# A graph network's first layer: the edge-score products with 128 moving columns instead of 64 and 1

## The reference

```
h = x @ W_w + W_b
row, col = (edge_index[0], edge_index[1])
e = h[row] @ a_src + h[col] @ a_dst + a_b
e = jax.nn.leaky_relu(e, negative_slope=0.01)
attention = jax.nn.softmax(e, axis=0)
msg = attention * h[col]
out = jax.ops.segment_sum(msg, row, num_segments=N_NODES)
```

## Time and profile before

| | |
|---|---|
| time before, median of 3 runs | 11837.31 us (11834.0 to 11841.89) |
| the profiled execution | 11841.19 us, span 11839.4 us |
| first weight load of line 556 to the last sum of this stage | 217.8 to 929.8 us |
| mean granted clock over the span | 0.742 |

### The profile page before, as it was taken

One profiled execution on the slowest core, in us unless ns is written; L12 is line 12 of the kernel. 1 busy time (PEld: TensorE's weight loads), 2 busy tenths in 40 slices (PEclk: granted clock), 3 DMA queues, 4 the chain that ended last, 5 costly groups with the idle time before them and its releaser, 6 DMA issues. The chain is left out here.

```text
span 11839.4 us, 182004 instructions
## 1 busy us (share of the span) xinstructions
PE 7849.9 (66%) x39163; PEld 6599.3 (56%) x39164; DVE 7062.0 (60%) x13587; ACT 2661.2 (22%) x8800; POOL 6678.2 (56%) x6703
## 2 busy tenths in 40 slices
PE   4995444437886377764654777563788778877886
PEld 3995444426775355542433666462566556655665
DVE  4445454444444289995675666566566656665666
ACT  1331000001111200004651000131333333333333
POOL 0006888846775077762322777330677667766776
PEclk6555666655555799997986666675899889988998
DMA  3114555543221167764532444330444344434444
GB/s 108 38 39 85 95 96 97 95 91 84 81 81 55 24 224 244 245 217 102 157 115 61 153 152 153 105 111 27 138 154 154 124 138 154 150 128 138 154 150 137
DMA packets 828292, 1435.96 MB, mean 121 GB/s; under 512 B 182864, under 2 KB 494268, under 8 KB 787760
## 3 DMA queue, kind: packets, MB, share of 16 engines
q1 hardware_dynamic: 531136, 981.94, 25.7%
q0 software_dynamic: 297072, 453.23, 17.0%
HBM read 1115.44 MB, written 320.07 MB: 121 GB/s over the span
## 5 line engine op out<-in xcount | busy, mean ns | idle before, releaser
L1614 POOL DMA_INDIRECT T<-gather_d,srci x2508 | 2459.3, 981 | 1263.4 <-issue 755.6
L827 POOL DMA_INDIRECT added_d<-T,slots x832 | 1296.3, 1558 | 281.5 <-issue 219.7
L1198 PE MATMUL PS<-T,ident 128*128 128x256 f32 (+1 forms) x3328 | 1069.2, 411 | 453.8 <-DMA T<-wide_d,srci 244.7
L1147 POOL DMA_INDIRECT T<-wide_d,srci x832 | 860.4, 1034 | 673.5 <-PEq L71 420.1
L1147 POOL DMA_INDIRECT T<-gather_d,srci x832 | 820.1, 986 | 531.7 <-PEq L71 278.3
L1196 PE MATMUL PS<-T 128*128 x3328 | 1004.3, 392 | 139.9 <-issue 98.5
L1418 PE MATMUL PS<-T 128*128 128x260 f32 (+1 forms) x3328 | 806.7, 403 | 424.0 <-DVEq L1471 349.6
L1198 PEld LDWEIGHTS PS<-T,ident 128*128 128x128 f32 x3328 | 672.4, 236 | 705.7 <-DMA T<-wide_d,srci 347.6
L940 POOL DMA_INDIRECT T<-gather_d,srci x832 | 792.8, 953 | 439.1 <-issue 253.7
L1397 POOL TENSOR_TENSOR T<-T,LG 128x256 f32<-128x256 f32 (+1 forms) x840 | 429.6, 532 | 998.6 <-PE PS L1418 753.7
L1418 PEld LDWEIGHTS PS<-T 128*128 128x128 f32 x3328 | 634.5, 240 | 596.2 <-DVEq L1471 329.8
(11 more groups left out here) (252 smaller groups left out, 16011.4 us busy)
## 6 DMA issues: line engine op xcount, KB each, us to landing
T<-quads_d SPq DMA_DIRECT2D x315, 1024.0 KB
T<-edge_rows_d SPq DMA_DIRECT2D x210, 512.0 KB
edge_rows_d<-T SPq DMA_DIRECT2D x209, 512.0 KB, 2.8
T<-onehot_t_d SPq DMA_DIRECT2D x416, 256.0 KB
T<-gather_d,srci POOLq DMA_INDIRECT x4172, 2.6
T<-edge_rows_d SPq DMA_DIRECT2D x210, 256.0 KB
onehot_t_d<-T SPq DMA_DIRECT2D x208, 256.0 KB, 3.4
edge_rows_d<-T SPq DMA_DIRECT2D x208, 256.0 KB, 2.1
```

The source lines that it names most:

```text
L827: gp.indirect_dma_start(added_d[u][:, :], bass.IndirectOffsetOnAxis(ap=slots[:, k:k + 1], axis=0), part(OUT[r], u), None, compute_op=ALU.a ...
L1147: gp.indirect_dma_start(part(R[n % RING], u, width), None, table[:, :], bass.IndirectOffsetOnAxis(ap=srci[:, k:k + 1], axis=0)).then_inc(r ...
L1198: last = T_.matmul(spot(i, u), ident[:, :], part(R[r], u, width), start=False, stop=True)
L1614: gp.indirect_dma_start(part(R[n % RING], u), None, gather_d[:, :], bass.IndirectOffsetOnAxis(ap=srci[:, k:k + 1], axis=0)).then_inc(rows_ ...
```

## The change

Both products of a step get 128 moving columns. The first takes all 128 columns of `S2` (the upper ones are zero in columns 49 to 127). The second takes 128 columns of `LG` from the step's block on. It is written from column 64 of the place in PSUM on, over the upper half of what the first wrote; its first column is the one that is used. A place in PSUM grows from 65 to 256 columns for a step, so four groups now take all eight banks. The mask reads 4 x 65 numbers with a stride of 256 in place of 260 in a row. Weights, loads, one-hot matrices, `pick`, sums and the number of instructions stay.

```
-        S2 = W[:, 5 * DIM:5 * DIM + LOW]
+        S2 = W[:, 5 * DIM:6 * DIM]
...
-            tcols = LG[:, 2 * ALL:2 * ALL + BLOCKS]
+            tcols = LG[:, 2 * ALL:2 * ALL + 2 * P]
...
-            spot = lambda r, u: bank(r)[:, u * both:(u + 1) * both]
+            room = 2 * P
+            spot = lambda r, u: PS[:, (r * GROUP + u) * room:(r * GROUP + u + 1) * room]
...
-                                T_.matmul(spot(r, u)[:, 0:LOW], part(LH[r], u), S2[:, 0:LOW], start=True, stop=True)
-                                last = T_.matmul(spot(r, u)[:, LOW:both], part(OT[r], u), tcols[:, bass.ds(bs[e % 2 * GROUP + u], 1)], start=True, stop=True)
+                                T_.matmul(spot(r, u)[:, 0:P], part(LH[r], u), S2, start=True, stop=True)
+                                last = T_.matmul(spot(r, u)[:, LOW:LOW + P], part(OT[r], u), tcols[:, bass.ds(bs[e % 2 * GROUP + u], P)], start=True, stop=True)
...
-                        V.tensor_tensor(PR[r % 2], bank(r)[:, 0:GROUP * both], EQ[r % 2], ALU.mult).then_inc(masked.h, 1)
+                        V.tensor_tensor(split(PR[r % 2], both), split(PS[:, r * GROUP * room:(r + 1) * GROUP * room], room)[:, :, 0:both], split(EQ[r % 2], both), ALU.mult).then_inc(masked.h, 1)
```

## The result

The changed kernel takes 11500.2 us (median of 4 runs, 11483.2 to 11508.1) against 11835.7 for the kernel before (4 runs, 11830.4 to 11841.9): a ratio of 0.9714 by the means of the runs, interval 0.9698 to 0.9731, and 335 us less by the medians. The direction and the main mechanism (the clock rises) are as forecast. The size is not quite: 317 us were predicted, and 11520 lies above what the interval allows (0.9731 x 11837 = 11519). The result sits on the lower edge of the range. The profiled execution took 11504.85 us, span 11503.1.

A forecast was written before the change was run, and what follows sets the result against it. TensorE's weight-load pitch at granted clock 0.50 was taken to bound the edge-score stage; 319.4 us gained at the high clock less 2.4 for its rise left -317, from 11837.3 to 11520 us, range 11498 to 11590.

The forecast's parts named there:

- What bounds the stage, and what 128 columns cost: Edge scores: TensorE alone sets the time, 0.213 us a record by its weight load; columns up to 128 are free.
- The clock rises: Edge scores: dense 128-column products with 128 rows lift TensorE's granted clock from 0.50 to 1.00.
- The group at the high clock: Edge scores: TensorE takes 1.784 us per group of 16 records, saving 1.628; VectorE, ScalarE and loads fit beneath.
- the upper bound of 2.26 us a group: Edge scores: pace if TensorE's instruction queue, at 56 ns an instruction, set it; 91 us more.
- The start of the stage: Until 266 us writes of zeros crowd DMA: 2.67 us a group, 16 groups done; stage's last product 319.4 us earlier.
- the prediction's own sign: Edge scores: the prediction counts as wrong if the stretch before 266 us holds many more than 16 groups.
- The rise of the clock: Edge scores: some 5 us at the low clock after TensorE's waits, half of them lost, taking 2.4 us off the gain.
- The rest does not move: Everything after the edge scores keeps its time, as nothing later shares the stage's data or its clock.
- another engine takes over: Rival: TensorE's queue or VectorE's waits set 1.9 to 2.26 us a group, 22 to 91 us more; chance 0.14.
- the clock stays: Rival: granted clock remains 0.50 in the edge scores and nothing changes, 11837 us; chance 0.05.
- the slower case: Rival: clock remains low and 128-column products take 0.251 us a record, 126 us more, 11963; chance 0.02.
- The variant without any hold-up by the zeros: Rival: all 208 groups run at 1.784 us, -335 us, 11502; counted as lower edge of the main case, 0.78.

The follow-up runs named there:

- e1: Changed kernel's PSUM places and strided mask, but products of 64 and 1 columns as before; 11851.7 us against 11855.3 for the kernel before.
- e2: Changed kernel with 128 columns in the source product only, the target product having 1; 11838.9 us against 11855.3 for the kernel before.
- e4: Changed kernel with 128 columns in both products but only 64 of the 128 rows; 11864.7 us against 11855.3 for the kernel before.
- e6: Changed kernel with the 64-row product of layer 1's edge stage given 128 rows, added ones zero; 12874.9 us against 12863.9 for the changed kernel.
- e0: The changed kernel run again, nothing altered; 12863.9 us against 13186.0 for the kernel before.
- e7: Changed kernel with the zeros cleared and written while layer 0's node product runs; 12832.6 us against 12831.2 for the changed kernel.
- e11: Changed kernel with two writes of zeros started with layer 0's node product, two with VectorE's sums behind it; 11510.7 us against 11518.1 for the changed kernel.
- e9: Changed kernel without TensorE's loads of block numbers, always taking block 0's columns; 12824.5 us against 12831.2 for the changed kernel.
- e3: Changed kernel with 128 columns in the target product only, the source product having 64; 11520.7 us against 11855.3 for the kernel before.

## Why the prediction was right or wrong

**What bounds the stage, and what 128 columns cost**: right. At 0.50 the pitch of a record is 0.213 us for 1, 64 and 128 columns (e1, e2, e4), at the high level 0.112 for 64 and 128 (predicted 0.1115). That it is the weight load's pitch fits, but no run changes the 128 columns of the load itself.

**The clock rises**: right, and the reason given (what moves, and not the busy share) is borne out by e1 to e4. That layer 1's stage spoke against it only through its 64 rows was a guess in the prediction; e4 shows that half the rows hold the clock at 0.50, and e6 that with full rows it leaves 0.50 in spite of the gaps. The gap as a sole cause falls; that it costs part of the way (0.69 and not 1.00) is not excluded.

**The group at the high clock**: right. 1.79 us against 1.784; no other engine took over. VectorE keeps 0.23 us. TensorE's queue is no bound where a register load takes 0.59 us, and the upper bound of 2.26 us a group did not come up.

**The start of the stage**: this step failed. "49 GB/s, so a pair of 0.262 MB takes 5.35 us, 2.67 us a group. That replaces 1.784 as the pace" made the stage 608.5 - 217.8 = 390.7 us, and 393.1 with the 2.4 us for the clock, from the first load to the end of the last product. It took 605.3 - 226.3 = 379.0. In e0, whose stage began at 218.9 us, 22 groups had been masked by 266 us, and not 16; from the first of these masks to the last are (265.86 - 222.78) / 21 = 2.05 us a group. By the prediction's own sign (many more than 16 groups before 266 us) this step was wrong.

It went wrong in two ways. First, the sum of 16 groups counts only the tables that arrive once the stage runs. The ring's four pairs, eight groups, had landed before it. DMA of the kernel before, 205 to 215 us, with eight loads of 128 KB:

```profile
q1 hardware_dynamic: 1152, 1.05, 36.0%
T<-step_at_d SPq DMA_DIRECT2D x4, 128.0 KB, 3.8
T<-step_lo_d SPq DMA_DIRECT2D x4, 128.0 KB, 4.1
```

With them, and with the prediction's own rate, (1.05 + 2.1) / 0.262 = 12 pairs or 24 groups are there by 266 us. The other 184 take 328.3 us, and the stage comes to 594.3 - 217.8 + 2.4 = 378.9 us. That this meets the 379.0 measured so closely is in part luck, since the rate was off too.

Second, the rate of 49 GB/s came from the earlier trace rows, 0.49 MB in ten us, and the queue could carry more. The changed kernel drew 0.60 from as crowded engines, between 235 and 245 us:

```profile
q0 software_dynamic: 667, 2.67, 82.2%
q1 hardware_dynamic: 655, 0.60, 20.0%
```

The kernel before needs a pair every 6.8 us, 0.38 MB in ten us. From 225 to 275 us it drew 0.32 to 0.53 in each ten us, while its TensorE waited for nothing: such a figure shows what was asked for. (The zeros' share of the DMA engines was also lower near the end than the prediction has it: 66.5% from 255 to 265 us in the earlier trace rows.)

The crowd did cost something: with the zeros elsewhere the stage is 374 us from first to last load (e7, e11), which is 208 x 16 x 0.1115 = 371.1 plus some 2.6 for the rise, and with them 378.3. So the term is 4 to 5 us and was put at 390.7 - 371.1 = 19.6. What it consists of can be partly other than I wrote: in that stretch the register loads on TensorE are slower too and one-hots are held up during GpSimd's issues. e9 shows that the register loads alone are not it; the shares are open.

**The rise of the clock**, 2.4 us: right (5.1 us at half speed).

**The rest does not move**: true of the mean, and careless for one pair of executions. The executions of the changed kernel differ by 21 to 32 us in a set of five, of which 8.5 us can come from layer 0's node product alone. Of the 18 us between 317 and the first 335, 14 are the stage's (331 us), by the mis-sized term, and the last 4 are within that scatter.

**The rivals**: that another engine takes over, that the clock stays, and the slower case did not happen. The variant without any hold-up by the zeros (-335 us) was nearest; that it meets the 335 us of the first medians is luck, since the stage gave 331.

## What to carry to other kernels

Where TensorE is full but its granted clock reads 0.50, look at what moves per weight load: with fp32 and a new 128x128 weight load for each product, columns up to 128 are free, and padding the moving side (or the rows) may buy the other clock level, here 331 us for no instruction more. Here 64 and 128 columns on full rows did so; 128 and 1 columns, or 128 columns on half of the rows, did not. Ask first whether TensorE sets the pace: in layer 1 the same lever raised the clock and gave nothing. Count what a ring has already loaded when a stage begins. A rate read from a queue that was not kept full is what was asked for and no limit, and it must not replace the pace of a faster consumer.

## What the runs showed that I had not expected

- The clock level does not follow the busy share: 300 of 300 us busy at 0.50 with 128 and 1 columns (e2), or with 128 columns and 64 rows (e4); 1.00 with 64 and 128 columns (e3).
- TensorE's register load takes 1.86 us in place of 0.59 while the DMA engines are full.
- One issue of a 3200 KB write on GpSimd holds a VectorE one-hot for 2.30 us in place of 0.48.
- Loose bursts, as in layer 0's node product, are at the high level for a different part of the time in each execution (mean clock 0.84 and 0.61 in the first two profiles); the first weight load of the next stage moves between 217.8 and 228.0 us in the kernels that write the zeros as before.
- The kernel before took 11848 us beside e11 and 13186 beside e0. Both sets are recorded under the same chip number, so what differs is open. For the changed kernel nearly all of the difference lies between the first and the last gather of the stages that have them (1311 of 1341 us between the first profile and e0), and the stage of the edge scores is 378 us in both.
